# Gathers of expert rows spread between the scatters, with a fifth buffer, in a routed feed-forward stage

## What is computed

```python
h = _layernorm(x, axis=-1) * (1 + cb) + sb
x = x + gb * ffn(h)

# ffn: N = 4096, D = 128, E = 8, F = 512, k = N / E = 512
route_prob = softmax(xf @ Ws + bs, axis=-1).T
route_vals, routes = top_k(route_prob, k)          # 512 tokens for each expert
xin = xf[routes]
h = gelu(einsum('ekd,edf->ekf', xin, W1) + b1[:, None, :])
out = einsum('ekf,efd->ekd', h, W2) + b2[:, None, :]
out = out * route_vals[..., None]
final = zeros((N, D)).at[routes.reshape(-1)].add(out.reshape(-1, D))
```

## Time and profile before

| | us |
|---|---|
| median of 3 runs | 391.67 (391.48 to 392.35) |
| the profiled execution | 388.7 |
| its span | 386.9 |
| TensorE busy | 264.5 |
| VectorE busy | 211.1 |
| GpSimd busy | 156.9 |
| ScalarE busy | 154.4 |
| first gather to last scatter's start, in that execution | 269.99 to 377.85 |
| mean granted TensorE clock | 0.855 of 2.4 GHz |

### The profile page before, as it was taken

How to read it: one execution, slowest core, us unless ns; L and a number is a source line. 1 busy time by engine, 2 the same in 40 slices (tenths; PEclk the granted TensorE clock), 3 DMA queues, 4 the chain that set the end, 5 groups by cost and what they waited for, 6 DMA issues and landing times.

```text
span 386.9 us, 8295 instructions
## 1 busy us (share of the span) xinstructions
PE 264.5 (68%) x3171; PEld 190.6 (49%) x3171; DVE 211.1 (55%) x715; ACT 154.4 (40%) x215; POOL 156.9 (41%) x209
## 2 busy tenths in 40 slices
PE   1879888889898898989875343324299987668000
PEld 1446666666566675667553232223166655645000
DVE  5566778867688776787664256666804222122100
ACT  5347554665645656455640044320043432022000
POOL 4104352350613406142241600000776888886661
PEclk9989999999999999999988565555579999699655
DMA  7507010010000100001010299940342433332321
GB/s 215 140 4 326 4 35 26 16 42 15 30 14 14 41 14 27 15 27 32 14 43 15 54 242 135 219 57 2 98 114 34 74 73 55 53 74 27 27 27 14
DMA packets 30543, 24.08 MB, mean 62 GB/s; under 512 B 6368, under 2 KB 27184, under 8 KB 30128
## 3 DMA queue, kind: packets, MB, share of 16 engines
q0 software_dynamic: 6848, 9.06, 15.0%
q1 hardware_dynamic: 23664, 14.59, 12.9%
HBM read 15.11 MB, written 8.54 MB: 61 GB/s over the span
## 4 chain that ended last, share of the span: by engine, by line
PE 27%; DVE 22%; POOL 21%; issue 12%; DMA 7%; ACT 7%; SPq 1%; DVEq 0%; POOLq 0%; ACTq 0%
POOL out_y L541 12%; PE ps L1115 6%; PE ps L1086 5%; POOL area L531 3%; DVE area L722 3%; ACT area L668 3%; ACT wgt L594 3%; DMA out_y<-o_sb,idx 3%; DMA modb<-mod_rows 2%; PE ps L1061 2%; DVE low L1001 2%; DMA wv_sb<-in_wv 2%; PE ps L1303 2%; PE ps L1157 2%; PE ps L1254 2%
## 5 line engine op out<-in xcount | busy, mean ns | idle before, releaser
L594 ACT ACTIVATE wgt<-ps 128x1024 f32<-128x1024 f32 x64 | 62.9, 1023 | 48.1 <-PE ps L1086 48.1
L541 POOL DMA_INDIRECT out_y<-o_sb,idx x32 | 50.5, 1578 | 18.5 <-issue 8.5
L531 POOL DMA_INDIRECT area<-token_rows,idx x32 | 31.0, 968 | 58.1 <-DVE idx L1014 48.7
L1115 PE MATMUL ps<-wgt,v_bd 128*32 128x259 f32 (+3 forms) x1024 | 44.1, 315 | 13.5 <-DVE y_t L754 8.3
L1086 PE MATMUL ps<-area 32*128 32x64 f32 (+3 forms) x1024 | 50.2, 321 | 3.4 <-ACT wgt L594 1.7
L1086 PEld LDWEIGHTS ps<-area 32*128 32x128 f32 x1024 | 42.2, 184 | 17.2 <-ACT wgt L594 10.5
L1115 PEld LDWEIGHTS ps<-wgt,v_bd 128*32 128x32 f32 x1024 | 30.6, 113 | 25.6 <-DVE y_t L754 9.8
L679 ACT ACTIVATE area<-ps,b_sb 128x512 f32<-128x512 f32 x32 | 21.9, 687 | 48.8 <-PE ps L1303 48.8
L482 POOL TENSOR_TENSOR x<-gated,xall 128x256 f32<-128x256 f32 x16 | 11.6, 726 | 66.9 <-DVE gated L775 66.9
L738 DVE SCALAR_TENSOR_TENSOR wgt<-wgt,mask 128x512 f32<-128x512 f32 x32 | 23.7, 739 | 21.9 <-ACT wgt L594 21.9
L1313 PE MATMUL ps<-modb,area 128*128 128x128 f32 x256 | 31.9, 285 | 2.1 <-ACT area L679 2.1
(11 more groups left out here) (175 smaller groups left out, 442.8 us busy)
## 6 DMA issues: line engine op xcount, KB each, us to landing
modb<-mod_rows SPq DMA_DIRECT2D x3, 1024.0 KB, 7.5
out_y<-x SPq DMA_DIRECT2D x16, 128.0 KB, 1.8
token_rows<-h SPq DMA_DIRECT2D x16, 128.0 KB, 1.9
token_rows<-gb_mod POOLq DMA_DIRECT2D x1, 2048.0 KB, 27.9
xall<-in_w SPq DMA_DIRECT2D x1, 2048.0 KB, 24.3
modb<-in_w SPq DMA_DIRECT2D x8, 256.0 KB, 16.7
xall<-in_x SPq DMA_DIRECT2D x2, 768.0 KB, 8.4
xall<-in_x SPq DMA_DIRECT2D x2, 256.0 KB, 4.9
```

What stands on the lines that cost most here:

```text
L531: eng.indirect_dma_start(out=xg[e % 4][:, j, :], out_offset=None, in_=rows[:, :], in_offset=bass.IndirectOffsetOnAxis(ap=idx[:, e, j:j + 1 ...
L541: eng.indirect_dma_start(out=out[:, :], out_offset=bass.IndirectOffsetOnAxis(ap=idx[:, e, j:j + 1].bitcast(u32), axis=0), in_=o_sb[e % 2][ ...
L594: k = nc.scalar.activation(wgt[bb][:, 2 * half:2 * half + 2, :, 0:256], ps[:, 2 * half:2 * half + 2, :].rearrange("p c (a q) -> p c a q", ...
L1115: k = mm(ps[32 * cc:32 * cc + 32, B_PV, j * BK:SEQ + (3 if j < 3 else 0)], v_bd[par][:, 4 * bb + j, 4 * qd + cc, :], blocks[j][:, cc, :], ...
```

## The change

The buffers of gathered rows become five; the fifth lies where `p_all` was. `gather` can issue a part of an expert's four DMAs. The order on GpSimd is written out: all gathers of experts 0 to 3 and two of expert 4 ahead of scatter(0), then three, two, two, two, two and three gathers between the groups of scatters, and none between scatter(6) and scatter(7).

```diff
--- before.py
+++ after.py
@@ -53,6 +53,7 @@
     EPS_DEN = 2e-12
     ROW = 2 * D + NE
     NC = 8
+    NXG = 5
     NACT = 1024
     SHIFTS = [27, 24, 21, 18, 15, 12, 9, 6, 3, 0]
 
@@ -125,8 +126,9 @@
         hits = area_b[:, 4 * NTOK - NTOK // 2:4 * NTOK]
         signs = area_b[:, 3 * NTOK:3 * NTOK + NACT]
         xg = [area_f[:, HALF + n * CT * ROW:HALF + (n + 1) * CT * ROW].rearrange("p (j r) -> p j r", j=CT)
-              for n in range(4)]
-        at = HALF + 4 * CT * ROW
+              for n in range(NXG - 1)]
+        xg.append(area_f[:, 0:CT * ROW].rearrange("p (j r) -> p j r", j=CT))
+        at = HALF + (NXG - 1) * CT * ROW
         g_sb = area_f[:, at:at + FC * CAP].rearrange("p (k s) -> p k s", k=FC)
         at += FC * CAP
         x_t = [area_f[:, at + n * CAP:at + (n + 1) * CAP] for n in range(2)]
@@ -297,7 +299,7 @@
         s_in = sem("inside_ready")
         s_tok = sem("token_ready")
         s_idx = sem("index_ready")
-        s_xg = [sem(f"gathered{n}") for n in range(4)]
+        s_xg = [sem(f"gathered{n}") for n in range(NXG)]
         s_xtp = sem("x_t_psum")
         s_xt = sem("x_t_ready")
         s_h1 = sem("hidden_psum")
@@ -522,15 +524,16 @@
             eng.dma_start(rows[:, D:2 * D].rearrange("(b n) d -> b n d", b=NB),
                           gb_mod[:, :].unsqueeze(1).broadcast_to([NB, SEQ, D])).then_inc(s_gbrow, 16)
 
-            def gather(e):
-
-                eng.wait_ge(s_idx, e + 1)
-                if e >= 4:
-                    eng.wait_ge(s_o, e - 3)
-                for j in range(CT):
-                    eng.indirect_dma_start(out=xg[e % 4][:, j, :], out_offset=None, in_=rows[:, :],
+            def gather(e, j0=0, j1=CT):
+
+                if j0 == 0:
+                    eng.wait_ge(s_idx, e + 1)
+                    if e >= NXG:
+                        eng.wait_ge(s_o, e - NXG + 1)
+                for j in range(j0, j1):
+                    eng.indirect_dma_start(out=xg[e % NXG][:, j, :], out_offset=None, in_=rows[:, :],
                                            in_offset=bass.IndirectOffsetOnAxis(ap=idx[:, e, j:j + 1].bitcast(u32), axis=0))\
-                       .then_inc(s_xg[e % 4], 16)
+                       .then_inc(s_xg[e % NXG], 16)
 
             def scatter(e):
 
@@ -548,12 +551,26 @@
                 eng.wait_ge(s_h2o[bb], 16 * UNITS + 16)
             eng.wait_ge(s_gbrow, 16)
             eng.wait_ge(s_pro, 16)
-            for e in range(3):
+            for e in range(4):
                 gather(e)
-            for e in range(NE):
-                if e + 3 < NE:
-                    gather(e + 3)
-                scatter(e)
+            gather(4, 0, 2)
+            scatter(0)
+            gather(4, 2, 4)
+            gather(5, 0, 1)
+            scatter(1)
+            gather(5, 1, 3)
+            scatter(2)
+            gather(5, 3, 4)
+            gather(6, 0, 1)
+            scatter(3)
+            gather(6, 1, 3)
+            scatter(4)
+            gather(6, 3, 4)
+            gather(7, 0, 1)
+            scatter(5)
+            gather(7, 1, 4)
+            scatter(6)
+            scatter(7)
             eng.wait_ge(s_sc, 16 * CT * NE)
 
 
@@ -1033,7 +1050,7 @@
                 eng.wait_ge(s_ob, e + 1)
                 if e >= 2:
                     eng.wait_ge(s_sc, 16 * CT * (e - 1))
-                g = xg[e % 4]
+                g = xg[e % NXG]
                 for j in range(CT):
                     k = nc.vector.scalar_tensor_tensor(o_sb[e % 2][:, j, :], o_b[:, j, :],
                                                        g[:, j, 2 * D + e:2 * D + e + 1], g[:, j, D:2 * D],
@@ -1283,13 +1300,13 @@
 
             def to_x_t(e):
 
-                eng.wait_ge(s_xg[e % 4], 16 * CT * (e // 4 + 1))
+                eng.wait_ge(s_xg[e % NXG], 16 * CT * (e // NXG + 1))
                 if e == 1:
                     eng.wait_ge(s_idx, 6)
                 if e >= 2:
                     eng.wait_ge(s_xt, e - 1)
                 for j in range(CT):
-                    k = tr(ps[:, 6 + e % 2, j * P:(j + 1) * P], xg[e % 4][:, j, 0:D], ident[:, :])
+                    k = tr(ps[:, 6 + e % 2, j * P:(j + 1) * P], xg[e % NXG][:, j, 0:D], ident[:, :])
                 k.then_inc(s_xtp, 1)
 
             to_x_t(0)
```

## The result

| | before | changed |
|---|---|---|
| median, us | 392.01 (6 runs, 391.48 to 393.48) | 408.75 (6 runs, 407.4 to 413.74) |
| ratio | | 1.0427, 95% interval 1.0383 to 1.0471 |
| profiled execution (span) | 388.7 (386.9) | 408.05 (406.3) |
| scatter(0) after the first gather | 22.30 | 27.66 |
| scatter(4) after the first gather | 73.01 | 70.15 |

The kernel is slower, as forecast, but by 16.7 us and not by 12.0; 408.75 lies outside the range. Medians in this text are of all runs, while ratios and their intervals leave out slow runs, those more than 1.5% above the fastest of the same kernel, so that a ratio can differ a little from the quotient of two medians.

What follows compares the result with a forecast made beforehand. The prediction took GpSimd's chain of gathers and scatters to bound the kernel from the first gather on. Its steps moved scatter(7) from 372.26 to 384.27, +12.0 us, giving 403.7 from 391.67; range 399.4 to 407.5.

Steps and rivals of the forecast that it cites:

- one stall before scatter(5): GpSimd, free at 344.72, waits until 353.24 for output 5, queued behind expert 6's last gather: 8.5 us.
- one before scatter(6): GpSimd waits for output 6, queued behind expert 7's last gather: scatter(6) at 374.50 instead of 364.64, 9.9 us.
- Rivals A: The gates bind but TensorE stays at or soon returns to 2.4 GHz: 399.9 us, +8.2; chance 0.10.
- B: At scatters 5 and 6 output e does not wait for gathers of e+1: faster, 385.3 us; chance 0.04.
- D: The stalls are smaller and eat just the gain, needing distances of about 5 us: no change; chance 0.02.
- the sum: All GpSimd steps up to scatter(7) together: it starts at 384.27 against 372.26, +12.0 us.
- Two more gathers in front: +0.39: Ahead of scatter(0), two gathers use up 2.42 idle us: scatter(0) at 292.68 instead of 292.29, +0.39 us.
- A landing is covered by two gathers, by 0.37: Between scatter groups 1 to 4, two gathers leave 4.46 us where the bare landing wait took 4.09.
- rival C: Two gathers do not cover a landing; at 1 us later, scatter groups lose 1.9 us: 405.6; chance 0.08.
- Output 5 at the lower clock: TensorE's output matmuls after the idle wait, priced at 5.24 us within the 11.12 from gather to scatter.
- My bound of 7.48: Upper end for the 32 output matmuls at the lower clock all through: +2.24 us each for two, giving 408.2.
- the base: The median of 391.67 us to which 12.0 was added; the profiled execution, 388.7, lay 3.0 below the median.

Runs made afterwards that it cites:

- third run of the changed kernel: The changed kernel without a further edit, run again on the third chip: 401.52 us, 1.0320 times the kernel before.
- 3,3,3,3,2,0,0: Changed kernel with these numbers of gathers behind scatter(0), scatter(1) and so on, 18 in front: 391.14 us (0.9946), again 387.24 us (0.9904).
- the pause: GpSimd waits for the eighth gather's landing: in the 3,3,3,3,2,0,0 order 387.02 us (0.9946), 393.36 (1.0102), 390.70 (one execution); in the kernel before 390.28 (1.0011).
- 12 in front: Changed kernel with twelve gathers ahead of scatter(0), then 5,3,4,4,4,0,0 behind the scatters: 394.04 us, 1.0000 times the kernel before.

## Why the prediction was right and wrong

**Right: the mechanism and where it sits.** Output e queued behind the gathers of e+1, one stall before scatter(5) and one before scatter(6), 8.5 and 9.9 forecast, 9.2 and 9.9 measured (the idle times of 9.52 and 10.15 without the 0.30 that stands between any two instructions); moving one gather removed one stall, moving both removed both, and swapping the order on TensorE and VectorE removed them too, but for 2.8 us before scatter(6). Rivals A (the clock stays high), B (no gate, 385.3) and D (stalls that just eat the gain) are out.

**Right: the sum, where nothing is held.** The changed kernel without the hold has scatter(7) at 114.14 where I had 114.28, and its steps agree too: scatter(0) at 22.67 (22.69), from there to scatter(4) 42.07 (41.90), to scatter(5) 18.69 (18.66), to scatter(6) 20.86 (21.26), to scatter(7) 9.85 (9.77).

**Wrong: the sum, where it is held.** Held profile against held profile, the distance of first gather and scatter(7) grew by 120.49 - 104.95 = 15.54 and not by 12.0. The 3.5 are:

- **"Two more gathers in front: +0.39"** is the step that failed. I took it that they use up the idle time in which GpSimd waits for expert 0. In a held execution that time is not to be had, because expert 0's result arrives behind the last gather: 27.66 - 25.01 = 2.65, so the term was 2.3 too small. Not held it is 22.67 - 22.30 = 0.37.
- **"A landing is covered by two gathers, by 0.37"**: not before scatter(2), which waited 0.87 instead of 0.30 us. Its predecessor's last scatter took 316.06 to 321.08, 5.02 instead of 4.46. With it scatters 0 to 4 took 42.49 where I had 41.90. This is rival C in small; in other profiles the same place idles up to 1.74.
- **Output 5 at the lower clock**: 5.89 instead of 5.24 us, 0.7 in scatter(5). My bound of 7.48 was not reached in any profile (6.22 at most), and the time that went with it, 408.2, lay above the range that I gave.
- Scatter(5) to scatter(6) took 21.23 (forecast 21.26), scatter(6) to scatter(7) 9.75 (9.77).

**Wrong, as it seems: the base.** "It lay 3.0 below the median of the runs" should have stopped me. The profiled execution of the kernel before was one without the hold; a held one has its scatter(7) 2.7 us later (104.95 against 102.27). The second, held profile of the same kernel took 391.28, close to the 391.67 to which I added 12.0. So that median stands, by all signs, for held executions, in which the two gathers cost more. The lowest times say the same. Of the kernel before no run is under 391.04 on the chip with the held profiles (44 runs) and none under 391.48 beside the changed kernel (6 runs), but 388.16 and 388.49 are reached on the other two chips; the changed kernel's lowest are 407.40 and 408.06 where its profile is held and 400.75 where it is not. It is not shown, as not every run has a profile here and chips may differ in other ways. From held to held, 15.5, one gets 407.2. The other 1.5 us up to 408.75 are open. In its profile the first gather starts 1.21 us later (271.20 against 269.99), which no edit touches; over all profiles that start lies between 269.64 and 275.01.

The third run of the changed kernel, not held in its profile, has a ratio of 1.0320 (1.0234 to 1.0405), which is 9 to 16 us: 12.0 lies in it, but four runs can't tell it from 15.5.

## What to carry to other kernels

Before scatters or stores are given cover by moving loads behind them, follow every engine's written order from the load: here a load gates not only its own expert but the output of the one before, and the distance it needs is read from one row of each engine (9.2 to 11.1 us; the two stalls showed 11.8 and 11.1). An idle gap that is used as free room has to be checked in more than one profile, and when the profiled execution is some us off the median of the runs, find out what those us are before a forecast is added to the median. The order 3,3,3,3,2,0,0 with 18 gathers in front wins one of the waits that the change can win and was a little faster than the kernel before, by 0.5 and 1.0%: 0.9946 (0.9903 to 0.9989) and 0.9904 (0.9863 to 0.9946).

## What the hardware showed unexpectedly

- **The hold.** With 16 to 20 gathers in front, in 11 of 19 profiles, the bias add of expert 0 starts on VectorE only 3.9 to 4.4 us after the last of these gathers has started (2.8 in the one held profile with the pause). In those 11 the increment of TensorE's semaphore is recorded 2.7 to 8.3 us after the end of the output matmuls of expert 0, in the others 0.01 to 0.02 us. Its cause is open: neither the chip nor a pause behind the eighth gather decides.
- **The hold goes with lost records.** The eight profiles without it hold 3325 to 3328 records of semaphore increments each, the eleven with it 3002 to 3082, and fewer from the first 10 us after the first gather on (54 to 68 instead of 119), long before expert 0 is late; up to the first gather all have 1902 or 1903. The profile with 12 in front has 3152, of them 60 in those 10 us, so by this sign it belongs with the held ones, and a hold may have passed there unseen. Whether what delays the signals also loses the records, or whether the recording of the profile itself delays them, no run here decides.
- **The clock behind an idle stretch.** After 0.99 and 1.59 idle us TensorE stayed at 2.4 GHz, after 3.66 it ran transposes at 1.2 GHz (1.12 us for four instead of 0.66). Between them the length alone does not decide: with 12 in front it ran four transposes in 1.12 us after 2.43 idle us and in 0.66 after 3.49. Output matmuls behind idle stretches of 4.5 to 12.7 us took anything from 4.64 to 6.22 us, so a single row (5.24) is a poor price for them.
- **Landings.** The last DMA of scatter(1) let the next group go only 5.0 to 5.9 us after its start (idle 0.87 to 1.74 behind two gathers), where the bare wait of later groups takes 4.1. It was this group in five profiles of four kernels; two other profiles with two gathers at this place, one of them of the changed kernel, show 4.5, and a third 4.7. Why is open.
